# Moving a softmax-attention's products two slots earlier beside another attention

## The chip, the cores and the metric

The kernel runs on one core of a Trainium2 chip. The metric is the device time of one execution in microseconds (us), as the median of several runs. The engines are PE (TensorE: matmuls and transposes), DVE (VectorE), ACT (ScalarE), POOL (GpSimd) and SP, which here only issues DMAs.

## The reference

Sixteen sequences of 512 tokens with 128 features go through four layers, each an attention-like block and a feed-forward block. Two blocks matter here. Layer 2's attention is causal softmax attention over 512 tokens with 16 heads of 8 features. Layer 3's feed-forward block begins with an attention of another kind: for each token alone, its 16 heads of 8 features attend to each other.

```
# layer 2, attention (q, k rotated; 16 heads of 8)
att = einsum('bhqd,bhkd->bhqk', q, k) / sqrt(dh)
att = softmax(where(causal, att, -inf))
y = einsum('bhqk,bhkd->bhqd', att, v)          # then the output projection
# layer 3, feed-forward: attention between the heads of one token
att = einsum('bthd,btgd->bthg', q, k) / sqrt(HD)
att = softmax(att)
out = einsum('bthg,btgd->bthd', att, v)        # then projection, norm, 8 gated experts
```

## The kernel before

The sequences are worked on in pairs (q is 0 or 1). The program has three parts: layer 0 up to layer 1's routing for eight pairs, a block for layer 1's experts, and then a loop of eight passes, one for each pair, with layers 2 and 3. The change lies in that loop. The head-to-head attention of layer 3 for a pair is not done in its own pass but in the next one, beside the layer 2 attention of the next pair. After the loop a last block does it for the last pair on its own.

**The layer 2 attention** (`twin_attention`) works on 8 quartets of heads (4 for each sequence of the pair). Every engine runs the same loop, `for c in range(-2, 9)` and in it `for u in range(6)`. A step (c, u) holds, on PE, transposed scores of quartet c (`scores_t`) and scores of quartet c+2 (`scores`), both into one ring of three PSUM buffers; on DVE the row maxima of quartet c+2 (`maxima`, L792); on ACT the exponents of quartet c; on POOL the causal mask of quartet c (`mask`, L597 and L601), which the product with the values on PE (`values`) waits for. At u = 1 PE turns the maxima of quartet c+1, and DVE adds them to the queries (`shift(c+1)`, L816). At u = 2 PE spreads the sums of quartet c-1 (`spread_sums`, L1852), which waits for `shift(c+1)`, since both use bank 7; ACT inverts them, and DVE divides at u = 3 (L808). PE takes its instructions in order, so what stands behind `spread_sums` waits too. Steps with c = -2 and -1 have scores and maxima alone; steps from c = 6 on have no scores and no maxima.

**The head-to-head attention** is spread over the same steps. It has 16 products m = 0 to 15, one POOL instruction of 2048 elements a partition each (`product`, L651): m = 0 to 7 multiply q and k (4 token tiles of each sequence), m = 8 to 15 weigh the values. DVE reduces each product in two halves (`take(m, half)`, L1364 for m below 8, L1367 from 8 on). Products alternate between two buffers, so product m waits until product m-2 is taken. DVE has six further pieces: `head_maxima(q)` (a reduction, then the subtraction L1378), `head_sums(q)` (a reduction and the reciprocal L1385), `head_outputs(q)` (the multiplication L1390). ACT has `head_exponents(q)`. In a step, DVE does `maxima`, then these pieces (`beside`), then `shift` or `divide`.

POOL does products 0 and 1 ahead of all masks. Then product 2+2c stands behind the mask of step (c, 1), and product 3+2c behind the last mask of quartet c, for c = 0 to 6. `TAKE_STEP` says in which step DVE takes which half.

Of the kernel before, what the change touches and what calls it, by code (L numbers as in the profile page):

```python
# [54 lines left out]
def program(nc, dram, x_in, out, sorted_x, sorted_y, kept_x, routes, returns, starts):  # L55
    with ExitStack() as ctx:
# [268 lines left out]
        for first, last in PARTS:  # L325
# [214 lines left out]
            with nc.Fori(0, SEQS // 2 if first < LAYERS else 1) as pair:  # L540
                sg = Signals()
                with nc.Block(no_gpsimd_drain=True) as block:
# [44 lines left out]
                    def _(pool):  # L587
# [79 lines left out]
                        def l2_masks():  # L667
                            for c in range(QUARTETS):
                                for u in range(STEPS_OF):
                                    mask("l2", c, u)  # L670
                                    if u == 1 and c < HEAD_QUARTETS:
                                        product(2 + 2 * c)
                                if c < HEAD_QUARTETS:
                                    product(3 + 2 * c)

                        if first == L2_ATTENTION:
                            l2_clear()
# [5 lines left out]
                        for layer in range(first, min(last, LAYERS)):  # L683
                            for of_layer, kind in enumerate(norms_of_layer[layer]):
                                if (layer, of_layer) == (LAYERS - 2, 2):
                                    for m in range(4 * len(PAIR)):
                                        pool.wait_ge(sg["l3_xc"], m + 1)
                                        fetch_rows(pool, sg, (4 + m,))
                                    for m in range(NT * len(PAIR)):
                                        pool.wait_ge(sg["l3_decay"], m + 1)  # L690
                                        fetch_rows(pool, sg, (12 + 2 * m, 13 + 2 * m))
                                for q in PAIR:
                                    pool.wait_ge(sg["stats_ready"], n + 1)
                                    if kind[0] == "ln":
                                        pool.tensor_scalar(VE[q][:], MV[q][:, :, 1], 1.0, kind[1], ALU.mult,  # L695
                                                           ALU.add).then_inc(sg["var_eps"], 1)
                                    else:
                                        pool.tensor_scalar(VE[q][:], SSQ[q][:], 1.0 / kind[2], kind[1], ALU.mult,
                                                           ALU.add).then_inc(sg["var_eps"], 1)
                                    pool.wait_ge(sg["var_eps"], n + 1)  # L700
                                    pool.tensor_tensor(RS[q][:], VE[q][:], minus_half[:],  # L701
                                                       ALU.pow).then_inc(sg["rstd_ready"], 1)
                                    n += 1
                                if (layer, of_layer) == (0, 1):
                                    for m in range(2 * QUARTETS):
                                        pool.wait_ge(sg["l0_probt"], m + 1)
                                        send_rows(pool, sg, (m,))
                                if (layer, of_layer) == (LAYERS - 2, 0):
                                    fetch_rows(pool, sg, (2, 3))
                                if layer == LAYERS - 1:  # L710
                                    fetch_rows(pool, sg, (28 + 2 * of_layer, 29 + 2 * of_layer))
                            if layer == L1_ATTENTION:
                                l1_masks()
                            if layer == L2_ATTENTION:
                                pool.wait_ge(sg["l2_v"], len(PAIR))
                                for m in range(2):
                                    product(m)
                                l2_masks()
                            if layer == L2_ATTENTION + 1:
                                finish_norms()  # L720
                                pool.wait_ge(sg["m_back"], 16)
                                fetch_rows(pool, sg, (0, 1))
# [9 lines left out]
                    def _(dve):  # L732
# [334 lines left out]
                        def l2_attention():  # L1067
# [18 lines left out]
                            def beside(c, u):  # L1086
                                if (c, u) in TAKE_STEP:
                                    take(*TAKE_STEP[c, u])
                                if (c, u) == (2, 1):
                                    head_maxima(0)  # L1090
                                if (c, u) == (3, 1):
                                    head_sums(0)
                                if (c, u) == (4, 1):
                                    head_maxima(1)
                                if (c, u) == (5, 1):
                                    head_sums(1)
                                if (c, u) == (6, 1):
                                    head_outputs(0)
                                if (c, u) == (8, 1):
                                    head_outputs(1)  # L1100
                            twin_attention("l2", beside)
                            for q in PAIR:
# [270 lines left out]
                        def head_maxima(q):  # L1373
                            sc = ht_sc[q].rearrange("p t h g -> p (t h) g")
                            red = ht_sm[q][:, 0]
                            dve.wait_ge(sg["f_read"], NT * (q + 1))
                            done(dve.tensor_reduce(red, sc, AX, ALU.max))  # L1377
                            dve.tensor_tensor(sc, sc, red.unsqueeze(2).broadcast_to([P, NT * H, H]),  # L1378
                                              ALU.subtract).then_inc(sg["f_sc"], 1)

                        def head_sums(q):
                            red = ht_sm[q][:, 1]
                            dve.wait_ge(sg["f_exp"], q + 1)
                            done(dve.tensor_reduce(red, ht_sc[q].rearrange("p t h g -> p (t h) g"), AX, ALU.add))
                            done(dve.reciprocal(red, red))  # L1385
# [27 lines left out]
                    def _(act):  # L1413
# [153 lines left out]
                        def l2_attention():  # L1567
# [14 lines left out]
                                              ).then_inc(sg["l2_rows00"], 16)  # L1582

                            def beside(c, u):
                                if (c, u) == (2, 3):
                                    head_exponents(0)
                                if (c, u) == (5, 0):
                                    head_exponents(1)
                            twin_attention("l2", beside)

# [758 lines left out]


QUARTETS = len(PAIR) * HG
HEAD_QUARTETS = 7
TAKE_STEP = {(-1, 1): (0, 0), (-1, 2): (0, 1), (-1, 4): (1, 0), (0, 0): (1, 1)}
for c_ in range(HEAD_QUARTETS):
    TAKE_STEP[c_ + 1, 0], TAKE_STEP[c_ + 1, 2] = (2 + 2 * c_, 0), (2 + 2 * c_, 1)
    TAKE_STEP[c_ + 1, 4], TAKE_STEP[c_ + 1, 5] = (3 + 2 * c_, 0), (3 + 2 * c_, 1)
STATE_BANK = ((4, 5, 4), (6, 7, 5))
ROWS_BANK = ((1, 5), (6, 7))

# [160 lines left out]
```

## Time and profile before

| | before |
|---|---|
| median of 3 runs | 6272.16 us (6266.48 to 6282.14) |
| profiled execution, its own time | 6282.14 us |
| its span, first to last instruction | 6280.5 us |
| PE, DVE, ACT, POOL busy | 74%, 60%, 30%, 34% |
| mean granted TensorE clock | 0.806 of full speed |
| the eight passes of the loop | about 2840 to 6142 us |
| layer 2 attention in the second pass | about 3264 to 3409 us |

A mean over the whole program says little of one stage. The rows below are therefore from one pass, the second, as instructions in order of time on one engine, with a few sums over stretches of it.

### The profile page before, as it was taken

To read this page: it belongs to the slowest core of one execution; us is meant where nothing else is said; L and a number is where in the kernel's file an instruction comes from. 1 tells how busy PE (TensorE), PEld (TensorE's weight loads), DVE (VectorE), ACT (ScalarE), POOL (GpSimd) and SP (SyncE) were. 2 spreads that over 40 slices of the span, in tenths; PEclk is the share of its full clock that TensorE was granted. 3 is DMA by queue.
4 is the path that set the end of the run, shared out by engine and by line. 5 is a ranking of instruction groups with operands and counts; after the bars stand their busy time and mean duration, and the time that the engine had idled before them with its cause. 6 is when DMAs were issued, how large, how long until landed. Compare 5 with 4: busy or idle time off the path is not lost. (4 is left out here: it accounts for less than half of the span.)

```text
span 6280.5 us, 94417 instructions
## 1 busy us (share of the span) xinstructions
PE 4643.8 (74%) x35752; PEld 2805.3 (45%) x35752; DVE 3740.2 (60%) x11081; ACT 1858.0 (30%) x2829; POOL 2166.5 (34%) x2704
## 2 busy tenths in 40 slices
PE   5978797979697878767767677687676775876763
PEld 3454445454444454443544534435444353453442
DVE  3546555555555555448567666586676755766664
ACT  2334242424242433333123122231232322312220
POOL 1223231313131313556135243261452522613425
PEclk9889898989898988887768768687777776777775
DMA  4000000000000000650000000000000000000000
GB/s 140 6 17 7 16 7 16 8 15 11 12 11 12 11 12 22 210 168 8 9 19 2 15 13 6 16 8 10 19 3 14 12 6 17 6 11 17 3 15 3
DMA packets 141904, 146.45 MB, mean 23 GB/s; under 512 B 31262, under 2 KB 126048, under 8 KB 141048
## 3 DMA queue, kind: packets, MB, share of 16 engines
q1 hardware_dynamic: 114280, 93.48, 5.1%
q0 software_dynamic: 18432, 37.79, 1.9%
q10 hardware_dynamic: 8736, 8.91, 0.4%
q8 instruction: 310, 5.08, 0.3%
q14 instruction: 146, 1.20, 0.1%
HBM read 69.64 MB, written 62.59 MB: 21 GB/s over the span
## 5 line engine op out<-in xcount | busy, mean ns | idle before, releaser
L792 DVE CUSTOM_DVE_ANT_0 twin<-twin,w_mask_row 128x512 f32<-128x512 f32 (+3 forms) x2048 | 953.0, 522 | 397.4 <-PE twin L1752 394.4
L1752 PE MATMUL twin<-arena 32*128 32x128 f32 (+3 forms) x4096 | 837.5, 538 | 40.9 <-DMA arena<-hres 15.8
L1770 PE MATMUL twin<-arena 32*128 32x128 f32 (+3 forms) x4096 | 789.3, 506 | 7.9 <-DVE arena L792 6.7
L1435 ACT ACTIVATE arena<-twin 128x768 f32<-128x768 f32 (+1 forms) x544 | 478.5, 881 | 659.7 <-PE twin L1781 388.0
L1770 PEld LDWEIGHTS twin<-arena 32*128 32x128 f32 x4096 | 362.7, 205 | 458.0 <-issue 295.4
L695 POOL TENSOR_SCALAR ve<-mv 128x4 f32<-128x4 f32 x128 | 27.4, 214 | 1513.7 <-DVE mv L752 1513.1
L321 POOL DMA_INDIRECT got<-sorted_y,back x288 | 280.6, 974 | 532.4 <-ACT ring L1641 263.2
L1752 PEld LDWEIGHTS twin<-arena 32*128 32x128 f32 x4096 | 369.7, 213 | 209.0 <-issue 118.5
L313 POOL DMA_INDIRECT sorted_x<-got,w_mo_first_slots x288 | 281.6, 978 | 470.4 <-DVE ring L866 300.9
L1705 PE MATMUL twin<-w_ident,b 128*128 128x128 f32 x328 | 88.7, 431 | 340.5 <-DVE b L773 335.1
L1793 PE MATMUL twin<-arena 128*32 128x128 f32 (+3 forms) x2944 | 305.4, 454 | 0.7 <-POOL arena L597 0.7
L792 DVE DVE_READ_ACCUMULATOR2_ANT arena<- 128x1 f32 x2048 | 295.5, 144 | 0.0
L597 POOL TENSOR_SCALAR_AFFINE_SELECT arena<-arena 128x256 f32<-128x256 f32 x352 | 146.0, 417 | 353.5 <-ACT arena L1435 353.3
L1705 PE MATMUL twin<-w_ident,a 128*128 128x128 f32 x192 | 50.2, 412 | 279.8 <-DVE a L759 279.0
L1435 ACT ACTIVATE ring<-twin 128x768 f32<-128x768 f32 (+1 forms) x224 | 195.9, 880 | 204.0 <-PE twin L1770 201.5
L2166 PE MATMUL twin<-w_l3f_we,arena 128*128 128x128 f32 x1152 | 219.2, 353 | 30.8 <-DVE arena L1115 30.8
L701 POOL TENSOR_TENSOR rs<-ve,minus_half 128x4 f32<-128x4 f32 x208 | 222.9, 1072 | 17.3
L2166 PEld LDWEIGHTS twin<-w_l3f_we,arena 128*128 128x128 f32 x1152 | 189.9, 252 | 79.2 <-DVE arena L1115 48.7
L1705 PEld LDWEIGHTS twin<-w_ident,b 128*128 128x128 f32 x328 | 60.9, 221 | 360.0 <-DVE b L773 354.4
L651 POOL TENSOR_TENSOR w_mo_wgu<-w_mo_wgu,w_l_cs_feat 128x2048 f32<-128x2048 f32 x36 | 197.2, 5480 | 62.4 <-DVE w_mo_wgu L1364 31.1
L651 POOL TENSOR_TENSOR w_mo_wgu<-w_mo_wgu 128x2048 f32<-128x2048 f32 x36 | 196.2, 5455 | 32.8 <-DVE w_l_wo L1367 23.3
L651 POOL TENSOR_TENSOR w_mo_wgu<-w_l_wo,w_l_cs_feat 128x2048 f32<-128x2048 f32 x36 | 161.4, 4496 | 100.7 <-DVE arena L1081 75.1
(440 smaller groups left out, 10467.1 us busy)
## 6 DMA issues: line engine op xcount, KB each, us to landing
sorted_y<-arena SPq DMA_DIRECT2D x96, 256.0 KB, 2.8
sorted_x<-zeros ACTq DMA_DIRECT2D x2, 4096.0 KB, 20.0
a<-sorted_x SPq DMA_DIRECT2D x64, 128.0 KB
b<-sorted_x SPq DMA_DIRECT2D x64, 128.0 KB, 2.4
hres<-sorted_x SPq DMA_DIRECT2D x64, 128.0 KB
sorted_x<-got,w_mo_first_slots POOLq DMA_INDIRECT x288
got<-sorted_y,back POOLq DMA_INDIRECT x288, 2.5
x_out<-w_l_w SPq DMA_DIRECT2D x18, 256.0 KB, 2.3
```

Of the source, the lines that this page charges most:

```text
L313: pool.indirect_dma_start(sorted_x[r % GROUPS], bass.IndirectOffsetOnAxis(ap=slot_of[:, q, n:n + 1], axis=0), normed[q][:, r // GROUPS], N ...
L321: pool.indirect_dma_start(got[q][:, n], None, sorted_y, bass.IndirectOffsetOnAxis(ap=back[:, q, n:n + 1].bitcast(U32), axis=0)).then_inc(s ...
L597: pool.affine_select(p, p, [[0, 2], [1, P]], ALU.is_ge, 0.0, base=0, channel_multiplier=-1).then_inc(sg[tag + "_masked"], 1)
L651: pool.tensor_tensor(pr, left.broadcast_to(shape), right.broadcast_to(shape), ALU.mult).then_inc(sg["f_pool"], 1)
L701: pool.tensor_tensor(RS[q][:], VE[q][:], minus_half[:], ALU.pow).then_inc(sg["rstd_ready"], 1)
L792: last = dve.tensor_tensor_reduce(s[:, e, at:at + w], s[:, e, at:at + w], W["mask_row"][:, T - w:T], -1.0, 3e38, ALU.add, ALU.min, into)
L1435: act.activation(at_pt[tag][n % len(at_pt[tag])][:, :, 0:w], twin[SLOT["scores_t", c, u] % 3][:, :, 0:w], ACT.Exp, scale=1.0 if tag == "l1 ...
L1705: i = pe.transpose(pb(q, b)[:, t * P:(t + 1) * P], src[:, t], ident)
L1752: last = pe.matmul(s[:, e, at:at + w], queries[r, P * i:P * (i + 1)], keys[r, 0:w], start=(at == 0), stop=True, skip_group_check=True)
L1770: last = pe.matmul(s[:, e, at:at + w], keys[r, P * m:P * (m + 1)], queries[r, P * m:T], start=(at == 0), stop=(tag == "l2"), skip_group_ch ...
L1793: last = pe.matmul(bank[into][rows_of(j), P * m:T], weights(m, j), at_pt[tag][n % len(at_pt[tag])][:, j % 2, at:at + w], start=(m == 0), s ...
L2166: i = pe.matmul(pb3(q, 3)[:, t], mo_fb[q][:, (e - 1) % 2, t * P:(t + 1) * P], weights[:, (e - 1) * P:e * P], start=(e == 1 and t == 0), st ...
```

## The change

Four products instead of two stand ahead of the masks, and all others follow one quartet earlier: `HEAD_QUARTETS` goes from 7 to 6, and product 4+2c stands where 2+2c stood. DVE's pieces move with them:

| piece | step before | step after |
|---|---|---|
| the 8 takes of m = 0 to 3 | (-1,1) (-1,2) (-1,4) (0,0) (1,0) (1,2) (1,4) (1,5) | (-2,3) (-2,4) (-1,0) (-1,1) (-1,2) (-1,3) (-1,5) (0,0) |
| takes of the others | four a quartet, c = 2 to 7 | four a quartet, c = 1 to 6 |
| `head_maxima` of 0 and 1 | (2,1) (4,1) | (0,1) (3,1) |
| `head_sums` of 0 and 1 | (3,1) (5,1) | (1,1) (4,1) |
| `head_outputs` of 0 and 1 | (6,1) (8,1) | (5,1) (7,1) |
| `head_exponents` of 0 and 1 (ACT) | (2,3) (5,0) | (0,3) (4,0) |

```
-                                        product(2 + 2 * c)
+                                        product(4 + 2 * c)
                                 if c < HEAD_QUARTETS:
-                                    product(3 + 2 * c)
+                                    product(5 + 2 * c)
...
-                                for m in range(2):
+                                for m in range(4):
                                     product(m)
...
-                                if (c, u) == (2, 1):
+                                if (c, u) == (0, 1):
                                     head_maxima(0)
+                                if (c, u) == (1, 1):
+                                    head_sums(0)
                                 if (c, u) == (3, 1):
-                                    head_sums(0)
+                                    head_maxima(1)
                                 if (c, u) == (4, 1):
-                                    head_maxima(1)
+                                    head_sums(1)
                                 if (c, u) == (5, 1):
-                                    head_sums(1)
-                                if (c, u) == (6, 1):
                                     head_outputs(0)
-                                if (c, u) == (8, 1):
+                                if (c, u) == (7, 1):
                                     head_outputs(1)
...
-                                if (c, u) == (2, 3):
+                                if (c, u) == (0, 3):
                                     head_exponents(0)
-                                if (c, u) == (5, 0):
+                                if (c, u) == (4, 0):
                                     head_exponents(1)
...
-HEAD_QUARTETS = 7
-TAKE_STEP = {(-1, 1): (0, 0), (-1, 2): (0, 1), (-1, 4): (1, 0), (0, 0): (1, 1)}
+HEAD_QUARTETS = 6
+TAKE_STEP = {(-2, 3): (0, 0), (-2, 4): (0, 1), (-1, 0): (1, 0), (-1, 1): (1, 1), (-1, 2): (2, 0), (-1, 3): (2, 1),
+             (-1, 5): (3, 0), (0, 0): (3, 1)}
 for c_ in range(HEAD_QUARTETS):
-    TAKE_STEP[c_ + 1, 0], TAKE_STEP[c_ + 1, 2] = (2 + 2 * c_, 0), (2 + 2 * c_, 1)
-    TAKE_STEP[c_ + 1, 4], TAKE_STEP[c_ + 1, 5] = (3 + 2 * c_, 0), (3 + 2 * c_, 1)
+    TAKE_STEP[c_ + 1, 0], TAKE_STEP[c_ + 1, 2] = (4 + 2 * c_, 0), (4 + 2 * c_, 1)
+    TAKE_STEP[c_ + 1, 4], TAKE_STEP[c_ + 1, 5] = (5 + 2 * c_, 0), (5 + 2 * c_, 1)
```

## Rows read from the trace of the kernel before

**Rows 1.** Busy time of each engine in stretches of the second pass.

```profile
core 0: us, PE busy (x) PEld busy (x) DVE busy (x) ACT busy (x) POOL busy (x), PEclk, DMA share, GB/s
3264.00:3409.00 145.00, 116.54 (x816) 51.84 (x816) 118.05 (x315) 58.29 (x75) 103.39 (x64) 0.81 0.04 7
...
3282.00:3289.00 7.00, 6.63 (x24) 2.53 (x26) 7.00 (x26) 2.05 (x2) 0.49 (x2) 0.50 0.12 23
3383.00:3409.00 26.00, 19.23 (x122) 7.25 (x122) 11.60 (x13) 11.88 (x17) 16.64 (x14) 0.76 0.00 1
```

**Rows 2.** DVE: first maximum of quartets 0 and 1, one group of takes.

```profile
3267.32 0.70 DVE L792 CUSTOM_DVE_ANT_0 twin<-twin,w_mask_row 128x512 f32<-128x512 f32 x1 [3.15 <-PE twin L1752]
...
3274.45 0.75 DVE L792 CUSTOM_DVE_ANT_0 twin<-twin,w_mask_row 128x512 f32<-128x512 f32 x1
...
L1364 DVE TENSOR_REDUCE w_mo_wgu<-w_mo_wgu 128x128 f32<-128x1024 f32 x16 | 19.5, 1219 | 0.0
```

**Rows 3.** DVE in order of time: the eight shifts of the second pass.

```profile
3278.18 0.70 DVE L816 TENSOR_TENSOR arena<-arena,twin 128x512 f32<-128x512 f32 x1
3289.21 0.68 DVE L816 TENSOR_TENSOR arena<-arena,twin 128x512 f32<-128x512 f32 x1
3300.39 0.68 DVE L816 TENSOR_TENSOR arena<-arena,twin 128x512 f32<-128x512 f32 x1
3316.03 0.68 DVE L816 TENSOR_TENSOR arena<-arena,twin 128x512 f32<-128x512 f32 x1
3332.32 0.69 DVE L816 TENSOR_TENSOR arena<-arena,twin 128x512 f32<-128x512 f32 x1
3350.57 0.67 DVE L816 TENSOR_TENSOR arena<-arena,twin 128x512 f32<-128x512 f32 x1
3366.89 0.69 DVE L816 TENSOR_TENSOR arena<-arena,twin 128x512 f32<-128x512 f32 x1
3383.45 0.68 DVE L816 TENSOR_TENSOR arena<-arena,twin 128x512 f32<-128x512 f32 x1
```

**Rows 4.** DVE in order of time: pieces of the head-to-head attention, last divide.

```profile
3314.88 1.23 DVE L1378 TENSOR_TENSOR w_mo_wgu<-w_mo_wgu 128x1024 f32<-128x1024 f32 x1
3331.73 0.55 DVE L1385 RECIPROCAL w_mo_wgu<-w_mo_wgu 128x64 f32<-128x64 f32 x1
3348.81 1.83 DVE L1378 TENSOR_TENSOR w_mo_wgu<-w_mo_wgu 128x1024 f32<-128x1024 f32 x1
3378.51 5.03 DVE L1390 TENSOR_TENSOR w_l_wo<-w_l_wo,w_mo_wgu 128x512 f32<-128x512 f32 x1
3408.66 0.69 DVE L808 TENSOR_TENSOR arena<-arena,twin 128x512 f32<-128x512 f32 x1 [7.42 <-ACT twin L1456]
```

**Rows 5.** POOL in order of time: products 2, 9, 13, 15, next masks.

```profile
3289.30 4.51 POOL L651 TENSOR_TENSOR w_mo_wgu<-w_l_wo,w_l_cs_feat 128x2048 f32<-128x2048 f32 x1
3344.09 5.47 POOL L651 TENSOR_TENSOR w_mo_wgu<-w_mo_wgu,w_l_cs_feat 128x2048 f32<-128x2048 f32 x1 [1.11 <-DVE w_mo_wgu L1364]
3377.55 5.43 POOL L651 TENSOR_TENSOR w_mo_wgu<-w_mo_wgu 128x2048 f32<-128x2048 f32 x1 [0.38 <-DVE w_l_wo L1367]
3392.68 5.46 POOL L651 TENSOR_TENSOR w_mo_wgu<-w_mo_wgu 128x2048 f32<-128x2048 f32 x1
3398.07 1.16 POOL L597 TENSOR_SCALAR_AFFINE_SELECT ring<-ring 128x256 f32<-128x256 f32 x3
```

**Rows 6.** PE in order of time, three waits; ACT, exponents of step (0, 1).

```profile
3316.81 1.86 PE L1852 MATMUL twin<-b,w_sel_sum 128*128 128x512 f32 x2 [3.52 <-issue]
3384.23 2.05 PE L1852 MATMUL twin<-b,w_sel_sum 128*128 128x512 f32 x2 [4.06 <-issue]
3398.92 1.94 PE L1793 MATMUL twin<-ring,arena 128*32 128x512 f32 x8 [1.83 <-POOL ring L597]
...
3287.83 1.02 ACT L1435 ACTIVATE arena<-twin 128x1024 f32<-128x1024 f32 x1 [2.51 <-PE twin L1770]
```

**Rows 7.** Three stretches and their granted clock, columns as in rows 1.

```profile
3290.00:3313.00 23.00, 21.77 (x206) 9.76 (x200) 20.77 (x70) 12.55 (x16) 20.25 (x14) 1.00 0.07 14
3313.00:3317.00 4.00, 0.48 (x5) 0.22 (x2) 3.97 (x8) 0.91 (x2) 3.38 (x3) 1.00 0.00 0
3317.00:3320.00 3.00, 3.00 (x10) 0.95 (x11) 1.83 (x5) 1.16 (x2) 1.08 (x1) 0.50 0.00 0
```

## The prediction

> **What bounds the kernel now.** I first read the busy share by stage, then one pass in order of time on DVE, because every moved piece but the products is DVE's. In the layer 2 attention of one pass DVE is busy for 118 of 145 us, PE for 117 [rows 1]. No engine is full over the whole stage, so the question is who is full where. There are three regions.
>
> *Head, up to the second shift.* In 3282 to 3289 DVE is busy for all 7.0 us, and PE runs at half its clock (0.50) [rows 1]. The maxima of one quartet take 7.1 us back to back (3267.32 to 3274.45) [rows 2]. So here DVE bounds, and all that is added to it is paid.
>
> *Middle.* The shifts follow each other after 11.0, 11.2, 15.6, 16.3, 18.3, 16.3 and 16.6 us [rows 3]; I call these intervals P0 to P6 (P0 from shift 0 to shift 1). A quartet with four takes and no further piece would need about 13.2 us: P2 is 15.6 and holds `head_maxima(0)`, whose reduction I put at 1.22 us like a take of the same input, and whose subtraction took 1.23 [rows 2, 4]; 15.65 - 2.45 = 13.2. PE waits at the end of each interval for the shift: 3.52 us ahead of 3316.81 [rows 6]. That wait costs again: the clock stays 1.00 through the gap of 3313 to 3317 and is 0.50 in the 3 us after it [rows 7].
>
> *Tail, from shift 7 (3383.45) to the end of the last divide (3409.35), 25.9 us* [rows 3, 4]. DVE is busy for only 11.6 of its 26 us [rows 1]. The stage is set by PE's order and by what PE waits for: 4.06 us for shift 7, and 1.83 us for masks of the last quartet [rows 6], which stood behind product 15 on POOL (3392.68 for 5.46 us, masks at 3398.07) [rows 5].
>
> So the change takes work out of a tail where DVE has room and POOL is in the way, and puts it into a head where DVE has none.
>
> **The change, part by part, for one pass** (changes in us).
>
> 1. *Ahead of shift 0.* The takes placed there go from 1 to 4. Three more at 1.2 us [rows 2]: **+3.6**. Products 2 and 3 now wait for takes 0 and 1, and all masks are queued behind them on POOL. By the steps, take 1 ends just before the shift at 3278.2 + 3.6 = 3281.8, so product 3 (4.5 us, as product 2 [rows 5]) is over at 3286.3. The first masks need exponents of (0,0) and (0,1), the latter today at 3287.8 [rows 6] and then some 3.6 later. No cost; if product 3 came 3 us later, the first masks would be late by about 1 us.
>
> 2. *P0.* Four takes instead of three, +1.2. `head_maxima(0)` enters, +2.45. Its subtraction reads both inputs from SBUF, and so did three instructions that ran beside a product: L1390 began at 3378.51 and ended 0.56 us after product 13 (3377.55 + 5.43 = 3382.98; 3383.54), against some 0.7 of own work; L1378 at 3348.81 ended at 3350.64, 1.08 after product 9's end at 3349.56 [rows 4, 5]. The takes beside the same products did not lengthen. Product 4 will stand where product 2 stood, 1.5 us after the exponents of (0,1) began (3287.83, 3289.30) [rows 5, 6]. These move with maxima (1,5), by 3.5 to 4 us, so the product runs from about 3293 to 3297.6. DVE reaches the subtraction at about 3295: shift 1 would start at 3289.2 + 3.6 + 1.2 = 3294.0 without the piece, plus 1.2 for the reduction. It is held for 2.4 us. P0: 1.2 + 2.45 + 2.4 = **+6.1**. Bounds for the hold: 0 if the product is later or is already over, 4.5 if it starts just ahead.
> The Trainium skill, page "SBUF — State Buffer", section "Who interferes with whom", says that a DVE instruction with two SBUF inputs and a GpSimd instruction that reads SBUF exclude each other for the whole instruction, and that `tensor_reduce` on trn2 never contends. By that rule the hold is the whole remainder of product 4; if two such instructions only shared bandwidth, the hold would be near 1 us and the pass 1.4 us better. The trace agrees with the page: 5.03 us for L1390 [rows 4].
>
> 3. *P1.* `head_sums(0)` enters: 1.22 + 0.55 = 1.8 [rows 2, 4]. P1 is 11.2 us, and DVE's work in it is 7.1 + 1.2 + 0.7 = 9.0, so there is room for it, if PE keeps up. But PE has run dry during the hold (three score buffers), for about 3 us, and such a gap brought half clock for 3 us [rows 7]. I take **+1.0**; bounds 0 and +5 (PE at half clock through much of P1).
>
> 4. *P2.* `head_maxima(0)` leaves: **-2.4**. With it PE's wait ahead of shift 3 shrinks from 3.5 to about 1 us, and the fall of the clock there should go too.
>
> 5. *P3.* `head_sums(0)` (1.8) gives way to `head_maxima(1)` (2.45, and 0.6 of hold beside product 9 as now [rows 4, 5]): +1.25. The clock stays up, so the 1.6 us that P3 now has beyond 13.2 + 1.8 - 0.3 goes: **-0.3** in sum.
>
> 6. *P4.* It holds `head_sums(1)` in place of `head_maxima(1)`, which makes it like today's P3: 18.25 becomes 16.3, **-1.9**.
>
> 7. *P5.* `head_sums(1)` (1.8) gives way to `head_outputs(0)`. Today that begins 1.0 us after product 13 and takes 5.03 [rows 4, 5]. In its new place two steps of maxima stand between as well, 2.4 us at a sixth of 7.1 each [rows 2], so 5.43 - 1.0 - 2.4 = 2.0 us of the product are left, and 0.6 of its own: 2.6 in all. **+0.8**.
>
> 8. *P6.* `head_outputs(0)` leaves it. DVE has no maxima in (6,0) and (6,1), and PE had done all ahead of `spread_sums` when it began its 4.06 us wait, at about 3380.2 [rows 6]. The interval shrinks until PE sets it. Shift 7 can follow PE's turn of the maxima, two PE steps ahead of 3380.2, at about 3378.7: 16.6 becomes 11.8, **-4.8** (bounds -3 and -5).
>
> 9. *Tail.* With shift 7 no longer late, `spread_sums(5)` starts at 3380.2 in today's time. Product 15 now stands where 13 stood (over at 3383.0 [rows 5]), so `values` of quartet 6 still waits for two masks, until about 3383.9. PE's 19.2 us of the tail were run at a clock of 0.76 [rows 1], so they are 14.6 at full clock; I take it that 2.6 of these (the spread and two score steps) come ahead of that point. That leaves 12.0 of work, 1 us of small waits, and about 4 us by estimate from the end of the values to the end of the divide: 3400.9. Counted from shift 7 at 3378.7, the tail is 22.2 instead of 25.9: **-3.7** (bounds -1.8, the wait alone, and -5.5). Four takes (4.9 us) also leave it, which is worth nothing, since DVE idles for 14 us there.
>
> 10. *Elsewhere.* `head_exponents` moves on ACT, which is busy for 58 of 145 us [rows 1]: nothing. No DMA moves. The block after the loop is untouched.
>
> Sum of a pass: 3.6 + 6.1 + 1.0 - 2.4 - 0.3 - 1.9 + 0.8 - 4.8 - 3.7 = -1.6. For eight passes -13, and some -5 more by estimate, because falls of the clock become fewer (five gaps a pass today, three after) and some last longer than the 3 us used. The profiled execution took 6282.1, so 6264 for it. A gap today costs 1.5 to 3 us in half clock (3 us at 0.50 [rows 7] is 1.5), so two gaps fewer are up to 24 us over the passes, of which parts 4 to 9 hold most. It stood 10 us above the median of the runs, so the median becomes **6254**.
>
> **Rivals.**
>
> *A. The head's price is not given back (slower).* At the hold PE runs dry, falls to half clock and stays there for all of P1, as it does today from 3282 to 3289 [rows 1]. P1 then costs +5 instead of +1, and shift 2 is late by 15 us instead of 11. The pass is at +2 to +3, the time 6272 + 20 = 6292. It decides from a P1 of about 14.5 us on. For it: nothing in the head lets DVE catch up. Against: PE was at half clock and dense for 7 us ahead of the full clock that today begins at 3290 [rows 1, 7].
>
> *B. Costs and gains cancel.* If the tail only loses the 1.83 us wait and P6 gains 3, the pass is at +1.6 - 1.8 = 0: 6272.
>
> *C. No hold at (0,1).* The same rule of exclusion, but product 4 starts after the subtraction, or the subtraction is through first. Then P0 gains 2.4, PE doesn't run dry and P1 costs 0: 3.4 better a pass, 6254 - 27 = 6227. Against: product 4 needs only exponents and one mask, which today give it a start 0.1 us after shift 1.
>
> **How the numbers follow.** My forecast gets 0.50 (own range 6242 to 6268), A 0.20, B 0.17, C 0.13. A measurement of this kernel can tell from no change what is over about 0.3%, or 19 us: 6253. The forecast lies at that line and, with its own range, gives 0.31 to faster, 0.16 to the same, 0.03 to slower; A gives 0.16 to slower and 0.04 to the same; B gives 0.14 to the same, 0.01 to faster and 0.02 to slower; C gives 0.13 to faster. That is 0.45, 0.34, 0.21. The range reaches from C's side, 6228, to A's, 6292.
>
> **What the profile would show.** Right: shift 0 later by 3.6 us from the first maximum on (14.5 instead of 10.9), P0 near 17 with an L1378 of over 3 us beside a product; P2 near 13; P6 below 12.5 and L1390 of about 2.3 us in P5; a tail of 22 us with masks of quartet 7 straight behind their exponents. Wrong: L1378 at 1.2 us in P0 (C), P1 above 14 with half clock (A), or a tail that keeps 25 us although its POOL wait is gone. That last would mean that PE and ACT alone set it.

## The result and the profile after

The changed kernel is slower: 6305.69 us as the median of 7 runs (6293.46 to 6327.52), against 6269.3 us for the kernel before on the same chip (7 runs). The ratio is 1.0064, with a 95% interval of 1.0044 to 1.0086. The forecast was 6254 us. The result lies outside its range, and on the side to which I gave 0.21.

The page of the profile after shows the same work as before:

```profile
span 6300.7 us, 94417 instructions
PE 4653.8 (74%) x35752; PEld 2809.6 (45%) x35752; DVE 3740.7 (59%) x11081; ACT 1859.4 (30%) x2829; POOL 2168.2 (34%) x2704
```

The two profiled spans differ by 20 us, less than the medians (36 us), because the profiled execution of before entered the loop 15 us later (first maximum of the first pass at 2850.87 us, after 2835.87; the code ahead of it is the same). Inside the loop, the first maxima of two passes are 414.8 us apart before and 419.3 after. That is 4.5 us a pass and 36 us in eight, the whole difference of the medians.

The table has the intervals of the prediction as means over the eight passes, in us. Each is read from the starts of the shifts on DVE; "head" runs from the first maximum to shift 0, "tail" from shift 7 to the end of the last divide.

```
            head    P0    P1    P2    P3    P4    P5    P6  tail  attention
before      10.9  11.0  11.7  15.7  16.7  17.9  16.9  17.1  24.6  142.5
after       14.1  17.1  14.1  15.6  16.9  17.2  17.1  13.9  22.4  148.5
change      +3.3  +6.1  +2.4  -0.1  +0.2  -0.7  +0.2  -3.2  -2.2   +6.0
predicted   +3.6  +6.1  +1.0  -2.4  -0.3  -1.9  +0.8  -4.8  -3.7   -1.6
```

The attention lost 6.0 us a pass, and the rest of the pass gained 1.5, which I had put at nothing and did not follow up. The means hide that passes differ: P0 is 17.1 us in all eight, but P6 is 12.8 in four of them and 13.9 to 16.0 in the others.

The rows of the fourth pass show each step. These are DVE's in order of time; they answer to [rows 3, 4].

```profile
4112.84 0.67 DVE L816 TENSOR_TENSOR arena<-arena,twin 128x512 f32<-128x512 f32 x1
...
4126.19 3.83 DVE L1378 TENSOR_TENSOR w_mo_wgu<-w_mo_wgu 128x1024 f32<-128x1024 f32 x1
4129.95 0.67 DVE L816 TENSOR_TENSOR arena<-arena,twin 128x512 f32<-128x512 f32 x1
...
4143.52 0.55 DVE L1385 RECIPROCAL w_mo_wgu<-w_mo_wgu 128x64 f32<-128x64 f32 x1
4144.11 0.69 DVE L816 TENSOR_TENSOR arena<-arena,twin 128x512 f32<-128x512 f32 x1
...
4159.44 0.68 DVE L816 TENSOR_TENSOR arena<-arena,twin 128x512 f32<-128x512 f32 x1
4173.89 2.31 DVE L1378 TENSOR_TENSOR w_mo_wgu<-w_mo_wgu 128x1024 f32<-128x1024 f32 x1
4176.13 0.68 DVE L816 TENSOR_TENSOR arena<-arena,twin 128x512 f32<-128x512 f32 x1
...
4206.62 2.52 DVE L1390 TENSOR_TENSOR w_l_wo<-w_l_wo,w_mo_wgu 128x512 f32<-128x512 f32 x1
```

The subtraction L1378, 1.23 us alone in [rows 4], takes 3.83 us here. Two rows of POOL in the same pass, product 4 beside that subtraction and product 15 in the tail:

```profile
4124.46 4.48 POOL L651 TENSOR_TENSOR w_mo_wgu<-absorbed_q,w_mo_wgu 128x2048 f32<-128x2048 f32 x1
...
4220.86 5.50 POOL L651 TENSOR_TENSOR w_mo_wgu<-w_mo_wgu 128x2048 f32<-128x2048 f32 x1 [1.10 <-DVE absorbed_q L1367]
```

Product 4 ends at 4128.94, and the subtraction 1.08 us later at 4130.02, as it did beside product 9 in [rows 4, 5].

PE's order of time has the idle time that went before an instruction in brackets. The first row is PE's wait behind the hold; the others are `spread_sums`, which waits for shifts 2 to 6:

```profile
4131.73 0.80 PE L1770 MATMUL twin<-arena 32*128 32x256 f32 x2 [3.58 <-DVE arena L792]
4144.94 1.10 PE L1852 MATMUL twin<-a,w_sel_sum 128*128 128x512 f32 x2 [2.27 <-DVE arena L816]
4160.22 1.10 PE L1852 MATMUL twin<-b,w_sel_sum 128*128 128x512 f32 x2 [0.71 <-issue]
4176.90 2.04 PE L1852 MATMUL twin<-hres,w_sel_sum 128*128 128x512 f32 x2 [4.17 <-issue]
4193.33 1.45 PE L1852 MATMUL twin<-arena,w_sel_sum 128*128 128x512 f32 x2 [2.96 <-issue]
4209.84 1.10 PE L1852 MATMUL twin<-a,w_sel_sum 128*128 128x512 f32 x2 [3.56 <-issue]
```

The same rows of the kernel before in its fourth pass, for shifts 2 to 6:

```profile
4130.36 1.10 PE L1852 MATMUL twin<-a,w_sel_sum 128*128 128x512 f32 x2 [0.43 <-DVE arena L816]
4145.96 1.58 PE L1852 MATMUL twin<-b,w_sel_sum 128*128 128x512 f32 x2 [3.52 <-issue]
4161.98 1.10 PE L1852 MATMUL twin<-hres,w_sel_sum 128*128 128x512 f32 x2 [2.96 <-issue]
4180.12 1.60 PE L1852 MATMUL twin<-arena,w_sel_sum 128*128 128x512 f32 x2 [3.71 <-issue]
4196.16 1.10 PE L1852 MATMUL twin<-a,w_sel_sum 128*128 128x512 f32 x2 [2.96 <-issue]
```

The gap ahead of shift 3 shrank from 3.52 to 0.71 us, as forecast. A new one of 2.27 us stands ahead of shift 2 and another of 3.58 us in P0. The clock follows the gaps (stretches of the kernel after, columns as in [rows 1]):

```profile
core 0: us, PE busy (x) PEld busy (x) DVE busy (x) ACT busy (x) POOL busy (x), PEclk, DMA share, GB/s
4112.00:4135.00 23.00, 17.51 (x76) 8.17 (x76) 22.04 (x57) 5.53 (x6) 12.09 (x7) 0.50 0.12 24
4136.00:4146.00 10.00, 7.60 (x73) 2.76 (x66) 8.68 (x25) 4.26 (x5) 5.89 (x4) 1.00 0.00 1
4146.30:4152.90 6.60, 6.60 (x44) 3.65 (x44) 4.74 (x15) 2.56 (x4) 5.82 (x4) 0.50 0.01 2
4153.00:4176.00 23.00, 17.93 (x166) 7.44 (x158) 22.15 (x58) 11.12 (x14) 19.56 (x11) 1.00 0.00 1
4222.00:4245.00 23.00, 17.35 (x142) 7.12 (x134) 7.30 (x9) 13.19 (x19) 9.95 (x13) 0.93 0.00 1
```

TensorE is at 0.50 (1.2 GHz) for all of the 23 us behind shift 0, through P0 and the first 6 us of P1. Before, [rows 1, 7] have it at 0.50 until 3289 and at 1.00 from 3290, some 12 us behind shift 0. It is at 1.00 (2.4 GHz) for 10 us, falls behind the 2.27 us gap, and is at 0.50 again for the 6.6 us from 4146.3 to 4152.9, in P2. It is so in seven of the eight passes. In the sixth it rises 12 us behind shift 0 and is at 0.50 again from 15.7 to 22.5 us behind it, around the gap that the hold makes; P1 is 13.9 us there. The tail of the fourth pass runs at 0.93; before it was at 0.76 in the second pass [rows 1] and at 0.89 in the fourth.

### The profile page after: what moved, and what is told of

It is laid out like the page before. It is cut to its first block and busy times, and to the rows that moved or that the text cites. A ratio compares the mean times of both kernels' runs of the same rounds, so it can differ in the third digit from the quotient of the medians.

```text
span 6300.7 us, 94417 instructions
## 1 busy us (share of the span) xinstructions
PE 4653.8 (74%) x35752; PEld 2809.6 (45%) x35752; DVE 3740.7 (59%) x11081; ACT 1859.4 (30%) x2829; POOL 2168.2 (34%) x2704
## 5 line engine op out<-in xcount | busy, mean ns | idle before, releaser
L1752 PE MATMUL twin<-arena 32*128 32x128 f32 (+3 forms) x4096 | 852.6, 541 | 56.1 <-DVE arena L792 30.5
L1770 PE MATMUL twin<-arena 32*128 32x128 f32 (+3 forms) x4096 | 811.6, 518 | 35.3 <-DVE arena L792 34.1
L1770 PEld LDWEIGHTS twin<-arena 32*128 32x128 f32 x4096 | 372.7, 211 | 494.8 <-issue 288.4
L1752 PEld LDWEIGHTS twin<-arena 32*128 32x128 f32 x4096 | 378.4, 216 | 231.8 <-issue 114.8
L597 POOL TENSOR_SCALAR_AFFINE_SELECT arena<-arena 128x256 f32<-128x256 f32 x352 | 145.7, 416 | 296.2 <-ACT arena L1435 296.1
L701 POOL TENSOR_TENSOR rs<-ve,minus_half 128x4 f32<-128x4 f32 x208 | 222.7, 1071 | 17.3
L651 POOL TENSOR_TENSOR w_mo_wgu<-w_mo_wgu 128x2048 f32<-128x2048 f32 x36 | 196.6, 5465 | 49.1 <-DVE absorbed_q L1367 27.0
L651 POOL TENSOR_TENSOR w_mo_wgu<-w_mo_wgu,w_l_cs_feat 128x2048 f32<-128x2048 f32 x36 | 197.2, 5481 | 45.0 <-DVE w_l_wo L1367 28.3
L651 POOL TENSOR_TENSOR w_mo_wgu<-w_l_wo,w_l_cs_feat 128x2048 f32<-128x2048 f32 x36 | 160.8, 4478 | 128.4 <-DVE arena L1081 76.8
```

What stands on the lines that cost most here:

```text
L597: pool.affine_select(p, p, [[0, 2], [1, P]], ALU.is_ge, 0.0, base=0, channel_multiplier=-1).then_inc(sg[tag + "_masked"], 1)
L651: pool.tensor_tensor(pr, left.broadcast_to(shape), right.broadcast_to(shape), ALU.mult).then_inc(sg["f_pool"], 1)
L701: pool.tensor_tensor(RS[q][:], VE[q][:], minus_half[:], ALU.pow).then_inc(sg["rstd_ready"], 1)
L1752: last = pe.matmul(s[:, e, at:at + w], queries[r, P * i:P * (i + 1)], keys[r, 0:w], start=(at == 0), stop=True, skip_group_check=True)
L1770: last = pe.matmul(s[:, e, at:at + w], keys[r, P * m:P * (m + 1)], queries[r, P * m:T], start=(at == 0), stop=(tag == "l2"), skip_group_ch ...
```

## The experiments

After the result my theory was this. The hold in P0 and the work added to the head are paid in full; PE's new gaps in P0 and P1 keep or bring half clock, which eats what P2 should gain; and the end gains because the hold of `head_outputs(0)` and the POOL work are gone from it. The rivals were that the takes alone cost it, and that the end gains by one of its causes only. All ratios are to the kernel before on the same chip, with 95% intervals. The intervals quoted are means over eight passes unless one pass is named.

### e1: `head_outputs(0)` out of P6 alone

The kernel before, with the piece at the other end of the interval's shift:

```
-if (c, u) == (6, 1): head_outputs(0)
 if (c, u) == (8, 1):
+    head_outputs(0)
     head_outputs(1)
```

> The kernel before, with head_outputs(0) alone moved from step (6,1) to (8,1), ahead of head_outputs(1). Theory 'hold': what the change gained in P6 (17.1 to 13.9 us on average, 12.8 in its good passes) came from this one DVE instruction no longer waiting 4.3 us for product 13 ahead of shift 7, and not from the takes that left the tail. Then P6 falls from 17.1 to 12 to 13 us here too, L1390 is 0.7 us, and the time falls by 4 to 6 us a pass, 32 to 48 us (ratio 0.992 to 0.995). Rival: the products and takes in quartet 6 set the pace; then P6 stays above 15.5 us and the time moves by less than 10 us.

Measured 6303.74 us, ratio 1.0014 [0.9999, 1.0029]. P6 fell from 17.1 to 13.0 us, and the tail grew from 24.6 to 29.0. The sum of the two is 42.0 us, against 41.7 before. POOL in order of time, behind shift 7 (4208.77) of the fourth pass; L651 are products 13 and 14, L597 masks:

```profile
4207.73 5.50 POOL L651 TENSOR_TENSOR w_mo_wgu<-w_mo_wgu 128x2048 f32<-128x2048 f32 x1 [0.37 <-DVE w_l_wo L1366]
4213.19 0.40 POOL L597 TENSOR_SCALAR_AFFINE_SELECT arena<-arena 128x256 f32<-128x256 f32 x1
...
4213.94 5.40 POOL L651 TENSOR_TENSOR w_mo_wgu<-w_mo_wgu 128x2048 f32<-128x2048 f32 x1
4219.30 0.76 POOL L597 TENSOR_SCALAR_AFFINE_SELECT ring<-ring 128x256 f32<-128x256 f32 x2
```

and PE, `values` waiting for these masks:

```profile
4214.01 0.62 PE L1792 MATMUL twin<-ring,arena 128*32 128x512 f32 x2 [1.72 <-POOL ring L597]
4220.12 1.51 PE L1792 MATMUL twin<-ring,arena 128*32 128x384 f32 x8 [3.41 <-POOL ring L597]
```

The earlier shift is given back in the tail. PE waits 1.72 and 3.41 us for masks that stand behind products 13 and 14 (1.26 and 1.81 us in the fourth pass of before), and behind these waits it runs at half clock for 17 us:

```profile
4215.60:4232.60 17.00, 13.59 (x68) 4.55 (x61) 5.05 (x6) 6.83 (x9) 13.19 (x11) 0.50 0.00 0
```

In the fourth pass of before it is at 0.50 for 7 us there, from 4211.3 to 4218.1. Counted from shift 0, product 15 began 2.3 us earlier in e1 (112.8 us behind it, before 115.2), and still the last divide ended 1.5 us later (131.1, before 129.6). So the 5 us of `head_outputs(0)` [rows 4] were worth nothing by themselves, against what I expected. How much of the give-back is POOL's order and how much the clock, e1 doesn't separate.

### e2: the four early takes alone

The kernel before, with four products ahead of the masks and their eight takes in the steps that the change gives them; all else stays where it was:

```
-for m in range(2):
+for m in range(4):
...
-if u == 1 and c < HEAD_QUARTETS:        # and the same for product(3 + 2 * c)
+if u == 1 and 1 <= c < HEAD_QUARTETS:
...                                      # TAKE_STEP for m = 0 to 3 as in the change
-for c_ in range(HEAD_QUARTETS):          # takes beside quartet c_ + 1
+for c_ in range(1, HEAD_QUARTETS):
```

> The kernel before, with only the early part of the change: products 2 and 3 ahead of the masks and their takes in steps (-2,3) to (0,0) as in the changed kernel, no product and no take in quartet 0 and 1's old places, all from product 4 on where it was, and head_maxima(0) left at (2,1). Theory 'head work': the four early halves cost 1.1 us each in a stretch where VectorE is full (3.3 us ahead of shift 0, 1.1 in P0) and give it back in P2, which loses three takes; P0 12.2, P1 11.5, P2 12.5 us, the pass at +0 to +2 us, the time at +0 to +16 us. Theory 'clock': the fuller head alone keeps TensorE at half clock beyond the second shift, P1 is over 13 us, and the pass is at +3 to +5 us, the time at +24 to +40 us.

Measured 6346.46 us, ratio 1.0067 [1.0043, 1.0092]. The head lost 3.3 us and P0 1.1. The takes of products 2 and 3 are gone from the steps of quartet 1. Three of them, 3.7 us, lay in P2, and P2 shrank from 15.7 to 14.9 us only, with 12.3 us of DVE's work left in it (fourth pass): DVE now waits for PE there. P3, P6 and the tail lost 0.9, 0.8 and 1.7. So takes that leave a middle interval are gained in small part, and takes that enter the head are paid in full. Both theories had less than was measured, which is the whole loss of the change (1.0067, the change 1.0064). The mean mixes two kinds of pass. In four the clock rose some 12 us behind shift 0, P1 was 10.2 and the attention 144 to 147 us; in the other four it rose after 20, P1 was 13.2 and the attention 153. What decides between them no run shows.

### e3: the maxima two steps later

The kernel after, with `head_maxima(0)` taken past product 4, and its exponents two steps later with it:

```
-if (c, u) == (0, 1): head_maxima(0)
+if (c, u) == (0, 3): head_maxima(0)
...
-if (c, u) == (0, 3): head_exponents(0)
+if (c, u) == (0, 5): head_exponents(0)
```

> The changed kernel, with head_maxima(0) moved from (0,1) to (0,3), behind the end of product 4, and its exponents on ScalarE from (0,3) to (0,5). Theory 'hold': the 2.6 us for which L1378 waits for product 4, and the 3.6 us gap on TensorE that comes of it, are what makes the change slower. Then L1378 is 1.2 us, P0 is 12.2 us instead of 17.1, P1 at most 14.5, and the pass is 4 to 6 us better than in the changed kernel: the time is that of the kernel before within 10 us. Theory 'head work': only the 2.6 us themselves come back, the time stays 15 to 20 us above the kernel before.

Measured 6284.36 us, ratio 0.9983 [0.9967, 0.9998]. P0 is 12.1 instead of 17.1 us in every pass, P1 15.2 instead of 14.1. DVE in order of time, the fourth pass:

```profile
4122.10 0.68 DVE L816 TENSOR_TENSOR arena<-arena,twin 128x512 f32<-128x512 f32 x1
4134.21 0.68 DVE L816 TENSOR_TENSOR arena<-arena,twin 128x512 f32<-128x512 f32 x1
4138.97 1.67 DVE L1378 TENSOR_TENSOR w_mo_wgu<-w_mo_wgu 128x1024 f32<-128x1024 f32 x1
4150.94 0.69 DVE L816 TENSOR_TENSOR arena<-arena,twin 128x512 f32<-128x512 f32 x1
```

The subtraction takes 1.67 us instead of 3.83. Moving one piece by two steps turns the change from 0.6% slower to 0.2% faster, so the place of this piece decides the sign. The hold is half of it: of the 5.0 us that P0 to P2 lost together, 2.6 are the hold. The other 2.4 are that P1 takes the piece in for 1.1 us where P0 paid 2.45, and that P2 is 13.3 us in three of the passes.

### e4: PE's gap behind the hold filled

The kernel after, with eight matmuls of constants at step (0, 3), which nothing reads:

```
+if (c, u) == (0, 3):
+    for n in range(8):
+        pe.matmul(bank[6], W["ones_b"], W["mask_row"], start=True, stop=True, ...)
```

> The changed kernel, with eight more bf16 matmuls (128x128 by 512, into a bank that nobody uses at that time) on TensorE in step (0,3), where it has its gap of 3.6 us. They compute nothing that is used. Theory 'clock': the clock of the stretch behind the gap is low because TensorE had run dry; with the gap filled it rises some 5 us earlier, P1 falls from 14.1 to 12 to 12.5 us, and the time is 12 to 20 us below the changed kernel. Rival: P1 is 14 us because of the order of VectorE's and TensorE's work alone, or the eight matmuls delay the scores by what they give back; the time stays within 8 us of the changed kernel.

Measured 6313.14 us, ratio 1.0036 [1.0017, 1.0055]. By the ratios that is 0.28% under the changed kernel, where 12 to 20 us were expected, but the intervals of the two overlap. P1 went from 14.1 to 13.6 us only, and P2 from 15.6 to 14.8. The passes say more than these means. In six of them the eight matmuls ran early, at full clock, in 1.9 us; 2.6 to 3.2 us of the gap remained, the clock fell there, and P1 was 13.7 to 14.6. In the fifth and the eighth they ran at half clock and filled the gap, the clock didn't fall there, and P1 was 12.6. So half clock at the gap is a part of P1's excess, though this rests on two passes.

P2 shows the price of the clock alone. DVE's work in it is the same (12.8 to 13.1 us), and so is the gap of 2.27 us ahead of it. P2 of the fifth, the fourth and the third pass, columns as in [rows 1]:

```profile
4580.93:4594.18 13.25, 11.48 (x102) 5.14 (x102) 12.84 (x39) 6.35 (x9) 9.92 (x6) 1.00 0.01 2
4166.67:4180.80 14.13, 12.84 (x102) 5.84 (x102) 12.85 (x39) 6.56 (x9) 9.91 (x6) 0.88 0.01 2
3746.64:3763.83 17.19, 16.36 (x98) 7.30 (x98) 13.13 (x39) 5.65 (x7) 11.28 (x8) 0.60 0.01 1
```

It is 13.25 us at a mean clock of 1.00, 14.1 at 0.88 and 17.2 at 0.60. P2 of the changed kernel's fourth pass lies between, 15.3 us at 0.78.

### e5 and e6: products 14 and 15, and their takes, left out

Two kernels from the one before. e5 leaves out products 14 and 15 and their takes in the loop; e6 leaves out the takes alone. In both, the head-to-head outputs lack the last two token tiles of the second sequence, and `head_outputs(1)` no longer waits for the takes that are left out.

```
-HEAD_QUARTETS = 7                    # e5: products and takes
+HEAD_QUARTETS = 6
...
-for c_ in range(HEAD_QUARTETS):      # e6: takes alone
+for c_ in range(HEAD_QUARTETS - 1):
```

> The kernel before without products 14 and 15 and their takes in the loop; in the loop, the last two token tiles of the second sequence of each pair lack their head-to-head outputs (the block after the loop is whole). head_outputs(0) stays at (6,1), so P6 keeps its hold. Theory 'POOL tail': what the change gained at the end (P6 and tail together 41.7 to 36.3 us) is that masks of quartets 6 and 7 no longer stand behind products; then P6 and tail here are 36 to 38 us, and the time is 30 to 45 us below the kernel before (ratio 0.993 to 0.995). Rival: the end is set by TensorE, ScalarE and shift 7; then the sum stays above 40 us and the time within 12 us.

> The kernel before with all its products, but without the four half takes of products 14 and 15 in the loop (steps (7,0) to (7,5)); the same outputs lack as in e5. Theory 'POOL tail': VectorE has room at the end, so the takes cost nothing; P6 and tail stay at 41 to 42 us and the time is that of the kernel before within 8 us. Rival 'VectorE tail': the takes delay divide and what waits for it; then the sum falls below 39 us and the time by 20 us or more.

e5 measured 6229.33 us, ratio 0.993 [0.9906, 0.9955]; e6 6272.77 us, ratio 0.9994 [0.9975, 1.0013]. P6 and tail together are 37.6 us in e5, 42.2 in e6 and 41.7 before. So the takes at the end cost nothing and the products cost 4.1 us a pass. On POOL, e5 has the end of the changed kernel: product 12 at step (5, 1), product 13 behind quartet 5, and none later. The change gained 5.4 us there (3.2 + 2.2). By e5, POOL's order gives 4.1 of them with the hold left in place (P6 is still 17.3 us in e5). The other 1.3 came with the hold gone as well, which alone gave nothing (e1).

### e7 and e8: PE's gaps ahead of the shifts filled

The kernel before (e7) and after (e8), with ten such matmuls in `spread_sums(c)`, ahead of its wait for the shift. Ten take some 2.3 us at full clock (nine in 2.11 us in the trace of e7).

```
+for n in range(10 if c in (1, 2, 3, 4, 5) else 0):   # e8: c in (0, 2, 3, 4)
+    pe.matmul(bank[6], W["ones_b"], W["mask_row"], start=True, stop=True, ...)
```

> The kernel before with ten bf16 matmuls (128x128 by 512) on TensorE, which compute nothing that is used, ahead of each wait of spread_sums(c) for the shift, c = 1 to 5. They stand in the gaps of 3 to 4 us. Theory 'clock': the stretches at half clock behind these gaps cost 1.5 to 2.5 us each; with the gaps filled P3, P4, P5 and P6 fall to 14.5 to 15.5 us, the pass by 4 to 7 us, the time by 32 to 56 us (ratio 0.991 to 0.995). Rival: VectorE sets these intervals and the half clock is hidden; the time moves by less than 10 us, or rises by what the filler delays.

> The changed kernel with the same ten matmuls ahead of the wait of spread_sums(c), c = 0, 2, 3 and 4, where it has gaps of 2.3, 4.2, 3.0 and 3.6 us. Theory 'clock': P2 is 15.3 us rather than the 13.2 us that I had forecast because the gap of 2.3 us ahead of shift 2 brings half clock; filled, P2 is 13.0 to 13.5 us in most passes, the slow passes with P5 or P6 of 16 to 18 us are gone, and the time falls by 30 to 60 us against the changed kernel, to the kernel before or below it. Rival: P2 stays above 15 us.

e7 measured 6225.88 us, ratio 0.9932 [0.9908, 0.9957]; e8 6263.74 us, ratio 1.0006 [0.9988, 1.0023]. Stretches of e7 from shift 2 to shift 6 of the fourth pass:

```profile
4099.00:4115.00 16.00, 13.70 (x112) 6.16 (x114) 15.55 (x42) 7.60 (x10) 13.11 (x10) 1.00 0.01 3
4115.00:4130.00 15.00, 13.58 (x112) 6.02 (x113) 14.58 (x41) 7.79 (x10) 11.68 (x8) 1.00 0.00 1
4130.00:4147.00 17.00, 13.59 (x111) 5.95 (x112) 16.61 (x40) 6.86 (x9) 13.59 (x8) 1.00 0.00 1
4147.00:4162.00 15.00, 13.49 (x111) 6.05 (x112) 14.58 (x41) 7.79 (x10) 12.48 (x6) 1.00 0.01 2
```

and of the kernel before, from shift 3 to shift 6:

```profile
4145.00:4161.00 16.00, 12.94 (x102) 5.82 (x102) 14.63 (x41) 7.89 (x10) 12.07 (x9) 0.89 0.00 1
4161.00:4179.00 18.00, 14.44 (x102) 6.83 (x102) 15.72 (x41) 6.99 (x9) 13.68 (x8) 0.81 0.00 1
4179.00:4195.00 16.00, 12.96 (x102) 5.81 (x102) 14.61 (x41) 8.01 (x10) 13.37 (x8) 0.89 0.00 2
```

With ten more matmuls in each stretch the clock is 1.00 instead of 0.81 to 0.89 and the intervals are shorter: P3 15.0 instead of 16.7, P5 15.4 instead of 16.9. The tail is 25.8 instead of 24.6. P2 stays 15.7 in e7: there DVE's own work, with `head_maxima(0)` in it, fills the interval. In e8 that piece is gone from P2, and with the gap ahead of shift 2 filled, P2 is 13.2 us in all eight passes, not 15.6. DVE of e8, fourth pass, shifts 0 to 3:

```profile
4090.02 0.67 DVE L816 TENSOR_TENSOR arena<-arena,twin 128x512 f32<-128x512 f32 x1
4103.36 3.85 DVE L1378 TENSOR_TENSOR w_mo_wgu<-w_mo_wgu 128x1024 f32<-128x1024 f32 x1
4107.13 0.67 DVE L816 TENSOR_TENSOR arena<-arena,twin 128x512 f32<-128x512 f32 x1
4121.70 0.69 DVE L816 TENSOR_TENSOR arena<-arena,twin 128x512 f32<-128x512 f32 x1
4134.89 0.68 DVE L816 TENSOR_TENSOR arena<-arena,twin 128x512 f32<-128x512 f32 x1
```

The -2.4 of the prediction's part 4 is there after all (15.6 to 13.2), once the clock holds. The hold and a P1 of 14.1 us stay.

In the sixth pass of e8 the clock is at 1.00 from P2 to the end. P6 and the tail of that pass:

```profile
5006.64:5018.30 11.66, 8.83 (x74) 4.18 (x78) 10.39 (x32) 5.00 (x7) 9.49 (x8) 1.00 0.01 1
5018.30:5038.79 20.49, 15.72 (x142) 6.35 (x141) 6.82 (x9) 13.65 (x20) 9.61 (x13) 1.00 0.00 1
```

They are 11.7 and 20.5 us, 9.5 less than in the kernel before (17.1 and 24.6), where parts 8 and 9 had 8.5. This sets single passes against a mean, but one pass of e9 and two of e10 have the same two values, also at 1.00.

### e9, e10, e11: both cures, and the head's gaps

e9 is the kernel after with e3's move and e8's matmuls, c = 0 to 4. e10 is e9 with two more matmuls in each step from (-1, 2) to (0, 1). e11 is e7 with these same two.

```
+if (-1, 2) <= (c, u) <= (0, 1):      # e10, e11
+    for n in range(2):
+        pe.matmul(bank[6], W["ones_b"], W["mask_row"], start=True, stop=True, ...)
```

> The changed kernel with head_maxima(0) at (0,3) and its exponents at (0,5), as in e3, and ten filling matmuls ahead of the wait of spread_sums(c), c = 0 to 4. If the price of the change is the hold at (0,1) plus the half clock behind the gaps, and its gain is POOL's work leaving the tail, then all three add up: P0 12.1, P1 14 to 15, P2 13.2, P3 16.7, P4 15, P5 16.2, P6 13, tail 22.5 us, together with 14.1 about 138 us a pass against 142.4 of the kernel before: 30 to 40 us faster (ratio 0.9935 to 0.9955), like e7. Rival: holding and clock overlap, so that the sum is no better than e8, ratio 1.000.

> e9 with two more filling matmuls on TensorE in each of the steps (-1,2) to (0,1), where it waits 0.3 to 1.1 us for maxima at half clock. Theory 'clock in the head': full clock comes earlier than today's 24 us after the first maximum, and P1 falls from 14 or 15 us to 12.5 to 13.5 us; 8 to 16 us faster than e9. Rival: VectorE sets P1 with head_maxima(0) and head_sums(0) in it, or the fillers delay the scores at half clock (0.43 us each by the granted clock); then the time is that of e9 within 8 us or above it.

> e7 (the kernel before, gaps ahead of the shifts filled) with the same two fillers in each of the steps (-1,2) to (0,1). In this kernel the head is set by VectorE alone up to shift 1 (10.9 and 11.0 us), so full clock there is worth nothing; the same as e7 within 8 us, or slower if the fillers delay scores. A gain of over 8 us would say that half clock in the head costs the kernel before as well.

| | time | ratio to before | P0 | P1 | P2 | attention |
|---|---|---|---|---|---|---|
| e9 | 6253.61 us | 0.9948 [0.9920, 0.9975] | 12.1 | 15.0 | 13.5 | 138.5 |
| e10 | 6244.64 us | 0.9927 [0.9906, 0.9949] | 12.6 | 15.4 | 13.6 | 138.2 |
| e11 | 6280.56 us | 0.9975 [0.9957, 0.9993] | 14.5 | 10.7 | 15.7 | 141.6 |

e9 came out as expected, so the two cures add up. The matmuls in the head don't shorten P1 (e10: 15.4 against 15.0), which was the theory of e10; its time is 9 us under that of e9, within the intervals of both. In e11 they lengthen P0 from 11.0 to 14.5 us: in a stretch without gaps they only stand ahead of the scores, at half clock. e10 (0.9927) and e7 (0.9932) are the fastest and not told apart. e7 is the kernel before with three lines added. So with the gaps filled the changed order has no lead over the old one that these runs can show (the attention is 138.8 us in e7, 138.5 and 138.2 in e9 and e10).

## Why the prediction was wrong

**Right.** Part 1 (+3.3 for +3.6). Part 2 to a tenth (+6.1): the hold, the place of product 4 and its length all came as worked out. The rule that the prediction cites from the Trainium skill, page "SBUF — State Buffer", section "Who interferes with whom", by which the subtraction waits out the whole product, agrees with the trace: 3.83 us, where the prediction's estimate for shared bandwidth gives near 2.2. (Part 2 speaks of three instructions held in the kernel before; it shows two.) Parts 8 and 9 have the right sign, and two thirds of their size (-3.2 and -2.2 for -4.8 and -3.7).

**Wrong, part 4: "the fall of the clock there should go too".** The gap ahead of shift 3 went as forecast, 3.52 to 0.71 us. But part 3 had put `head_sums(0)` into P1, and I costed it on DVE alone ("there is room for it"). It sits directly ahead of shift 2 and made PE's wait for that shift 2.27 us, where it was 0.43: its 1.8 us and the old wait make 2.2. The clock fell behind that gap instead, and P2 lost at 0.50 what it had been relieved of. P2 moved by -0.1 for -2.4. e8 shows this: the gap filled, P2 is 13.2. So does e4, where P2 is 13.25 with the gap unfilled in the three passes in which the clock didn't fall behind it.

**Wrong, part 10: "five gaps a pass today, three after".** Up to the tail of the fourth pass of after, PE has gaps over 2 us of 3.58, 2.27, 4.17, 2.96 and 3.56 us. These are five, as many as before (four in the rows above, and the one ahead of shift 7 [rows 6]). I struck off the two that the change relieves and added none for the pieces it places. The estimate of -5 us rested on that count. P3 (-0.3; measured +0.2) kept the clock at 1.00 up to its end, as I had it, but the subtraction in it took 2.31 us beside product 9, where it was 1.83 [rows 4]. P4 (-1.9; measured -0.7) became like the old P3, 16.4 us, in five passes; in the other three it was 18.4 to 19.0, with 10 to 14 us of it at 0.50. e8, with gaps filled, has P4 at 15.5 and P5 at 16.2.

**Too small, part 3.** P1 cost +2.4, not +1.0. The clock stayed at half for 23 us behind shift 0, not 12, in seven passes. Rival A named half clock in P1, but at +5 and as the whole of the loss; its own mark, a P1 from 14.5 us on, was not reached. The late rise isn't the only way to lose this. Where the clock rose after 11 to 12 us it fell again at the gap behind the hold, and P1 was 13.7 to 14.6 all the same (the sixth pass of after, six passes of e4, four of e8). Only the two passes of e4 with that gap filled have a P1 of 12.6, near what part 3 gave. What decides whether the clock rises 12 or 23 us behind shift 0 stays open.

**Parts 8 and 9, too large together.** I had -8.5 and measured -5.4. P6 did shrink because the hold of `head_outputs(0)` left it: e1, which moves that piece alone, has -4.1 there, and e5, which keeps it, has P6 at 17.3. But alone it is worth nothing (tail +4.4 in e1), while POOL's products alone are worth 4.1 (e5 and e6). What was missing from the sum is half clock again. Of the 12.8 us of P6 in the fourth pass of after, TensorE spent 6.8 at 0.50; in the sixth pass of e8, with none, P6 is 11.7 and the tail 20.5, and both parts are there in full.

By size, of the 7.6 us a pass between -1.6 and +6.0, P1 and P2 hold 3.7, P6 and tail 3.1, and P3 to P5 1.1. The hold, which I had right, is still the piece that could have been avoided (e3: from 1.0064 to 0.9983).

## What to carry to other kernels

When a piece moves in a schedule where TensorE waits at fixed points, write the list of TensorE's waits before and after, at every such point, the places that receive work above all: a wait that shrinks in one place and opens in another keeps the fall of the clock, and the move is worth nothing. Place an instruction of VectorE that reads two SBUF operands away from the long GpSimd instructions, by step; moving one such piece changed the sign here. Before crediting the end of a stage with the removal of its longest stall, ask what would be waited for next; e1 gave back in the tail all that P6 gained. And read the passes of a loop one by one beside their clock: the same work in P2 took 13.25 to 17.7 us in one trace, and the mean said little.

## What the runs showed of the hardware beyond expectation

- In the kernel after, the wait of 2.27 us on TensorE ahead of shift 2 was followed by half clock (0.50, 1.2 GHz) in all eight passes, in the fourth for 6.6 us. In e4 the same wait was followed by none in three passes, and P2 was 13.25 us there. A wait of this length brings half clock often, not always. Those of 0.43 and 0.71 us in the rows above were followed by stretches at 1.00.
- Ten small bf16 matmuls in each wait ahead of a shift, 2.3 us of work that nothing reads, kept the clock at 1.00 from shift 2 to shift 6 in six of eight passes and made the kernel before 0.68% faster (e7). The same kind of matmul in the dense head made it slower (e11 against e7: 0.9975 and 0.9932).
- Behind shift 0 the clock stayed at 0.50 for 23 us in seven passes of the kernel after, although PE was busy for 17.5 of them, and for 12 us in the sixth pass, with the same instructions. What decides between the two no run here shows.
